# The turned pair leaves PSUM in two halves, each with its own signal

## The reference, cut to what matters

```python
# layer 0: h = relu(layernorm(x))
x += relu( (D^-1 (alpha*adj + (1-alpha)*I) h) @ W0.T + b0 )
# layer 1: hyperbolic layer; two products with adj: adj @ (gamma * XW) and adj @ (gamma - 1)
# layer 2: h @ W2.T + b2, then per row of adj the maximum over its 32 largest entries' rows
# layer 3: adj (with the diagonal) normalised by row sums, times gamma * h; then tanh, logs, @ W3 + b3
```

## Time and profile before

| | |
|---|---|
| median of 3 runs | 3734.52 us |
| profiled execution, its own time | 3729.21 us |
| its span | 3727.4 us |
| granted TensorE clock, mean | 0.959 |
| TensorE busy, products and turns | 3344.1 us, 90% |
| ScalarE busy | 1618.0 us, 43% |
| VectorE busy | 2529.3 us, 68% |
| GpSimd busy | 2280.6 us, 61% |
| the copy L760 | 512 x 1.024 us = 524.1 us, idle before it 311.8 us |

### The profile page before, as it was taken

How to read it: one execution, slowest core, us unless ns; L and a number is a source line. 1 busy time by engine, 2 the same in 40 slices (tenths; PEclk the granted TensorE clock), 3 DMA queues, 4 the chain that set the end, 5 groups by cost and what they waited for, 6 DMA issues and landing times.

```text
span 3727.4 us, 75480 instructions
## 1 busy us (share of the span) xinstructions
PE 3344.1 (90%) x29444; PEld 3322.3 (89%) x29444; DVE 2529.3 (68%) x5448; ACT 1618.0 (43%) x3264; POOL 2280.6 (61%) x2023
## 2 busy tenths in 40 slices
PE   3999999999999999999999999950899998999873
PEld 2999999999999999999999999950899998999873
DVE  5588789788788788530256655645887878787834
ACT  2777777777877777431231212330121211121235
POOL 0999899898998999300075545526766666657100
PEclk9999999999999999999999999975999999999996
DMA  3999999999999999888899999941788898889751
GB/s 95 373 384 389 356 378 387 353 374 379 372 373 361 377 379 388 311 287 291 292 343 328 327 329 332 330 174 51 277 309 305 319 328 302 305 299 341 252 203 45
DMA packets 399660, 1155.04 MB, mean 310 GB/s; under 512 B 36605, under 2 KB 53950, under 8 KB 399358
## 3 DMA queue, kind: packets, MB, share of 16 engines
q1 hardware_dynamic: 359600, 1082.67, 78.8%
q0 software_dynamic: 31360, 64.29, 5.6%
q10 hardware_dynamic: 8398, 4.23, 0.4%
HBM read 874.19 MB, written 276.86 MB: 309 GB/s over the span
## 4 chain that ended last, share of the span: by engine, by line
PE 67%; DVE 20%; ACT 3%; issue 3%; POOL 3%; DMA 3%; DVEq 1%; SPq 0%; POOLq 0%; ACTq 0%
PE psT L661 18%; PE psU L578 18%; PE psT L702 11%; PE psT L566 9%; PE psU L661 6%; DVE agg L1474 4%; PE psU L702 3%; DVE HT L1470 3%; DMA adj_turned<-ATS 2%; DVE D L1302 2%; POOL D L470 2%; DVE W L1474 1%; DVE GR L1630 1%; POOL D L478 1%; ACT junk_rows L847 1%
## 5 line engine op out<-in xcount | busy, mean ns | idle before, releaser
L470 POOL TENSOR_TENSOR D<-D,iota 128x512 f32<-128x512 f32 x1024 | 1310.1, 1308 | 120.4 <-ACT D L767 98.1
L478 POOL DMA_INDIRECT D<-h_table,idx_own x640 | 624.7, 976 | 779.0 <-issue 509.1
L578 PE MATMUL psU<-HB,ATS 128*128 128x129 f32 x8192 | 1009.1, 277 | 35.9 <-ACT ATS L760 32.1
L578 PEld LDWEIGHTS psU<-HB,ATS 128*128 128x128 f32 x8192 | 961.4, 193 | 43.1 <-ACT ATS L760 36.4
L702 PE MATMUL psT<-ATS,PIECES 128*128 128x129 f32 x6144 | 786.1, 278 | 157.4 <-ACT ATS L927 102.4
L702 PEld LDWEIGHTS psT<-ATS,PIECES 128*128 128x128 f32 x6144 | 740.6, 195 | 162.5 <-issue 147.1
L1302 DVE MAX8 D<-D 128x8 f32<-128x512 f32 x1024 | 644.0, 683 | 262.6 <-POOL D L470 254.9
L661 PE MATMUL psT<-GR,PIECES 128*128 128x129 f32 x6144 | 772.4, 275 | 3.9 <-DMA PIECES<-adj_turned 3.9
L661 PEld LDWEIGHTS psT<-GR,PIECES 128*128 128x128 f32 x6144 | 729.7, 192 | 4.1 <-issue 4.1
L760 ACT ACTIVATE ATS<-psT 128x1024 f32<-128x1024 f32 x512 | 524.1, 1024 | 311.8 <-PE psT L566 220.6
L767 ACT ACTIVATE D<-PIECES 128x1024 f32<-128x1024 f32 x512 | 538.4, 1052 | 0.0
(11 more groups left out here) (381 smaller groups left out, 2693.4 us busy)
## 6 DMA issues: line engine op xcount, KB each, us to landing
PIECES<-adj_turned SPq DMA_DIRECT2D x512, 1024.0 KB
PIECES<-in_adj SPq DMA_DIRECT2D x256, 1024.0 KB
adj_turned<-ATS SPq DMA_DIRECT2D x512, 512.0 KB, 8.0
D<-h_table,idx_own POOLq DMA_INDIRECT x640
h_table<-HB ACTq DMA_DIRECT2D x8, 512.0 KB, 7.6
out_x<-X SPq DMA_DIRECT2D x2, 2048.0 KB, 8.7
D<-h_table,idx_pool POOLq DMA_INDIRECT x223
ATS<-h_table,idx_pool POOLq DMA_INDIRECT x117
```

The lines of the kernel that those rows point to most:

```text
L470: pool.tensor_tensor(key, key, iota[:, :], ALU.mult).then_inc(keyed, 1)
L478: pool.indirect_dma_start(slot, None, rows, bass.IndirectOffsetOnAxis(ap=index, axis=0)).then_inc(done, inc)
L578: last = nc.tensor.matmul(sum4(r), AT[K % NAT][:, b * GROUP + r * P:b * GROUP + (r + 1) * P], HB[:, j, :], start=(j == 0 and r % 2 == 0), ...
```

## The change

One copy of 1024 columns becomes two of 512. `pair_transposed` is raised after the fourth and after the eighth turn of a pair, and each half's copy waits for its own. `pair_copied` is raised by each half's copy, and the products of a half wait for that half alone. All other waits on the two semaphores have their numbers doubled, so that they still wait for the whole pair. The check that the buffer is free stays ahead of the first half.

```diff
--- before.py
+++ after.py
@@ -399,13 +399,13 @@
 
             def store_pairs(n):
                 for K in (2 * n, 2 * n + 1):
-                    sp.wait_ge(pair_copied, K + 1)
+                    sp.wait_ge(pair_copied, 2 * K + 2)
                     sp.dma_start(turned[K // NP, K % NP, :, :], AT[K % NAT]).then_inc(pair_stored[K % NAT], 16)
 
             for n in range(NPIECES):
                 if n >= SLOTS:
                     store_pairs(n - SLOTS)
-                    sp.wait_ge(pair_transposed, 2 * (n - SLOTS + 1))
+                    sp.wait_ge(pair_transposed, 4 * (n - SLOTS + 1))
                     sp.wait_ge(masked, 2 * (n - SLOTS + 1))
                     if (n - SLOTS) % NPC == 0:
                         sp.wait_ge(scanned, 2 * (n - SLOTS) + 1)
@@ -417,7 +417,7 @@
                 sp.wait_ge(piece_multiplied, q + 1)
                 sp.dma_start(slot_v[q % SLOTS], turned_v[s, k, :, :, :]).then_inc(piece_loaded[q % SLOTS], 16)
 
-            sp.wait_ge(pair_transposed, PAIRS)
+            sp.wait_ge(pair_transposed, 2 * PAIRS)
             sp.wait_ge(masked, 2 * NPIECES)
             for s in range(NSG):
                 for i in range(NAT):
@@ -559,21 +559,21 @@
                 if h == 0:
                     pe.wait_ge(piece_loaded[n % SLOTS], 16 * (n // SLOTS + 1))
                 if K >= 2:
-                    pe.wait_ge(pair_copied, K - 1)
+                    pe.wait_ge(pair_copied, 2 * K - 2)
                 for b in range(2):
                     x0 = h * 2 * P + b * P
                     for r in range(TPG):
                         last = nc.tensor.transpose(psT[h][:, b * GROUP + r * P:b * GROUP + (r + 1) * P],
                                                    pieces[n % SLOTS][:, r, x0:x0 + P], ident[:, :])
-                last.then_inc(pair_transposed, 1)
+                    last.then_inc(pair_transposed, 1)
 
             def add_pair(K):
                 g, k = K // NP, K % NP
-                pe.wait_ge(pair_copied, K + 1)
                 if g and k == 0:
                     pe.wait_ge(agg_copied, g)
                 for b in range(2):
                     j = 2 * k + b
+                    pe.wait_ge(pair_copied, 2 * K + b + 1)
                     for r in range(TPG):
                         last = nc.tensor.matmul(sum4(r), AT[K % NAT][:, b * GROUP + r * P:b * GROUP + (r + 1) * P],
                                                 HB[:, j, :], start=(j == 0 and r % 2 == 0),
@@ -643,7 +643,7 @@
                 nc.tensor.transpose(psY[0:PREFIX, P:2 * P], pfx[:, 1, :], ident[:, :]).then_inc(prefix_n, 1)
 
             def turned_pass():
-                pe.wait_ge(pair_copied, PAIRS)
+                pe.wait_ge(pair_copied, 2 * PAIRS)
                 pe.wait_ge(agg_copied, NG)
                 for s in range(NSG):
                     for k in range(NP):
@@ -753,11 +753,13 @@
                             .then_inc(hT_copied, 1)
 
             def copy_pair(K):
-                act.wait_ge(pair_transposed, K + 1)
                 if K >= NAT:
                     act.wait_ge(pair_used, K - NAT + 1)
                     act.wait_ge(pair_stored[K % NAT], 16 * (K // NAT))
-                nc.scalar.activation(AT[K % NAT], psT[K % 2][:, :], ACT.Copy).then_inc(pair_copied, 1)
+                for b in range(2):
+                    half = slice(b * GROUP, (b + 1) * GROUP)
+                    act.wait_ge(pair_transposed, 2 * K + b + 1)
+                    nc.scalar.activation(AT[K % NAT][:, half], psT[K % 2][:, half], ACT.Copy).then_inc(pair_copied, 1)
 
             def mask(K):
                 n, rows = K // 2, slice(K % 2 * KROWS, (K % 2 + 1) * KROWS)
```

## The result

The changed kernel took 3713.57 us (median of 4 runs, 3710.05 to 3717.77), the kernel before 3732.39 (4 runs, the three of before and one of 3730.25). The ratio is 0.9948, with a 95% interval of 0.9930 to 0.9965. By the medians the change is 18.8 us faster, by the interval 13 to 26. The forecast was 6 us faster, the range 3719 to 3738.

What follows compares the result with a forecast made beforehand. The first pass was taken to run at TensorE's pace, with DMA right behind. Long waits -1.5, short waits -4, seams -0.5 and pass end -0.4 gave about -6 us: 3723.2 profiled, 3728.5 as a median, range 3719 to 3738.

Steps and rivals of the forecast that it cites:

- The copy undisturbed: ScalarE's copy in ordinary first-pass pairs: first half starts 0.44 us earlier, store and mask move 0.36 ahead; 0 for TensorE.
- The seams: Between groups of the first pass, an earlier mask lets the sums' copy start sooner: 15 x 0.03, -0.5 us.
- rival 4: All gains of the first pass at their bounds: -13.8 us, giving 3720.7; chance 0.27, counted from 8 us on.
- The short waits: TensorE's 14 short first-pass waits for the copy, 7.1 us together, shrink by 0.3 each: -4 us.
- The long waits: Four first-pass waits behind VectorE's work, 29.3 us together, end 0.42 earlier each, less 0.05 for late masks: -1.5 us.
- Handling of signals: One more signal and one more wait on TensorE per first-pass pair cost 0, bounds -5 and +5 us.
- ScalarE's occupancy: Two half copies occupy ScalarE 0.99 us a pair against 0.92, 0.08 more, hidden in its idle time.
- End of the pass: The last mask comes 0.36 us earlier, so the second pass's first loads are issued earlier: -0.4 us.
- From a profile to a median: The same -6 us taken off the profiled execution, 3729.2 to 3723.2, and off the runs' median, 3734.5 to 3728.5.
- rival 1: ScalarE becomes the pace where it prepares layer 1 in the first pass: +6 us, giving 3740.6; chance 0.11.
- Rival 2: TensorE pays for the added signal or wait at the upper bound, +5 us, giving 3733.5; chance 0.20 together with Rival 3.
- Rival 3: DMA is near its limit, so TensorE's gain returns as later landings: 3734; chance 0.20 together with Rival 2.

Runs made afterwards that it cites:

- start_only: The changed kernel, except that TensorE's products wait for the whole pair's copy; the first half's copy still starts after four turns. Ratio 0.9981 to the kernel before.
- split_only: The changed kernel with two half copies, but the first waits for all eight turns and the products wait for the whole pair. Ratio 0.9996 to the kernel before.
- later_prep: The changed kernel with ScalarE's first squares of each preparation three pairs later: 4737.13 us against 4774.13 for the kernel before, ratio 0.9930.
- signals_only: The changed kernel with one whole copy after all eight turns; TensorE keeps the added signal and wait of each pair. Ratio 1.0005 to the kernel before.
- quarters: The changed kernel with four copies of 256 columns, each releasing its own products: 4745.76 us against 4753.12 for the kernel before, ratio 0.9987.
- the two timings with more runs: The changed kernel, unedited, timed twice more against the kernel before, nine runs each: ratios 0.9971 and 0.9975.
- mask_first: later_prep with ScalarE making a pair's mask ahead of its copy: 4711.72 us against 4753.12 for the kernel before; timed again, 4713.39 against 4751.32.

## Why the prediction was wrong

The direction was right and the two mechanisms in the sum are there. The size was a third to a half of what was measured, because one path was put at nothing and one term was too small. By that size the likeliest case was "no change that can be told".

- **The copy undisturbed, "None of it is on TensorE's path: 0": this step failed.** start_only has the earlier start without the earlier release, and gains 9 us (4 to 14). In the ledger it loses 46.4 us, where split_only, the same two copies without the earlier start, loses 53.1 (one profile each). The seams are one part of it: I bounded them by when the last products end and took 0.03 us each. Eleven of them lose 0.44 us instead of 0.58, 1.5 us together. The sums' copy follows the last products more closely: 178.10 is 1.98 us after 176.12, 2.07 before (178.60 after 176.53), where the mask held ScalarE. The larger part lies in the short waits. A copy that may start 0.36 us sooner leaves more time until TensorE needs it, and its store is issued sooner, in any pair and not only in the one that waits. That this is how the early start removes short waits is argued, not shown; rival 4 had named it.
- **The short waits: the mechanism right, the term mis-sized.** -4 us, from 7.1 us of waits. Four executions of each kernel have 7.0, 15.5, 8.0 and 7.7 us of them before, and 5.1, 1.0, 3.7 and 1.9 in the changed kernel (waits up to 3.5 us). The means are 9.6 and 2.9, so -6.6, or -5.5 with the late store's wait of 4.55 us in the first profile. This includes what the earlier start does. One profile was not enough to size a wait that depends on when stores land, and I allowed for that in rival 4 and not in the forecast's own spread.
- **The long waits: no evidence against the term.** -1.5 forecast, -0.6 by the ledger's means (-2.1 without the late store's wait), and a spread of 3 to 4 us between executions in either kernel, in which 0.42 each can't be read. That they come from where ScalarE waits for VectorE's rows is shown by later_prep. The prediction took more than four long waits as a sign that VectorE's chain had moved. It took waits of 5 us or less as the same sign. The first profile has a fifth, which a store caused, and behind it one for VectorE's rows of only 4.4 us. The three other profiles have four waits of 5.8 us or more, so that profile is the odd one and the sign doesn't hold.
- **Handling of signals: right for TensorE.** 0 forecast, +2 (-2 to +7) in signals_only, and a pair still costs 2.66 us. The 0.08 us by which the copy's start comes later was not foreseen.
- **ScalarE's occupancy: right, and smaller.** 0.97 us for two halves, not 0.99; split_only -2 (-6 to +2).
- **End of the pass: right.** 3.73 us for 3.89, -0.2 where -0.4 was forecast.
- **From a profile to a median.** I carried -6 over from the profiled execution to the median. The profiled execution of before was below every run of its kernel that the medians rest on, and the changed kernel's was the slowest of its four: the two profiled executions differ by 11.4 us and the medians by 18.8. In that pair the first pass gained only 4.8 us; the other 6.7 lie behind it, where the sum had nothing, and no experiment shows a cause for them.

The rivals: rival 1 is excluded for halves by split_only; quarters fit it, without showing it. Rival 2's +5 isn't excluded by the interval of signals_only, but the cadence gives no sign of it. Rival 3 is wrong in that gains are not returned. A store's median time from issue to landing is 8.3 us in the changed kernel's first profile against 8.0, but 8.1 to 8.2 against 8.0 to 8.1 in the later ones. Rival 4 (-13.8, 3720.7) was nearest: its sizes were about right for short waits and seams, not for the long waits.

The ledger's 9.6 us and the 12 to 14 us of the two timings with more runs agree within the intervals. What the first timing has beyond them stays open; its interval begins at 13.

## What to carry to other kernels

When an engine that sets the pace waits for another now and then, a copy cut into parts that signal for themselves can pay twice, by an earlier start and an earlier release, and each is worth measuring alone. Two parts are not four: here each added part cost the copying engine another 0.05 us a pair (0.92, 0.97 and 1.07 us for one, two and four parts), and four gained no more than two. Size occasional waits from several executions, not from one. A long wait behind an instruction that stands in order for someone else is better removed by moving that instruction (20 us here) than by shortening what follows it (1 or 2 us).

## What the runs showed of the hardware

TensorE's clock in the last stage rises at a time that differs between executions of the same kernel. Its products (L719) for the last unit before the rise and the first at the higher clock, in the changed kernel's first profile:

```profile
3645.26 2.08 PE L719 MATMUL psU<-W,HT 128*128 128x128 f32 x8 [0.73 <-ACT HT L982]
...
3648.93 1.16 PE L719 MATMUL psU<-W,HT 128*128 128x128 f32 x8 [0.73 <-ACT HT L982]
```

A unit's eight records take 1.16 us from 3648.93 on, 2.08 before. The granted clock is 0.50 (1.2 GHz) from 3631.0 to 3648.5, with TensorE busy 14.36 of 17.5 us, and 1.00 (2.4 GHz) from 3649.5 to 3675.0. The rise came 14.6 to 40.2 us after the stage's first products over 17 profiles, and these products span 47.4 to 52.9 us with it. The two executions of mask_first have 47.4 and 52.1: 4.7 us of difference that have nothing to do with an edit.

In a pair of eight turns and eight products, one more signal and one more wait of TensorE leave the pair at 2.66 us. But the copy that waits for the last turn's signal starts 0.08 us later (0.28 us after the products in signals_only, 0.20 in the kernel before).
